# Second layer's feed-forward: the hidden levels of 15 of 16 tiles transposed by DMA instead of by TensorE

## The reference, cut to what matters

```python
def activation_quant(x, num_bits=8):
    s = qp / jnp.clip(jnp.max(jnp.abs(xf), axis=-1, keepdims=True), EPS, None)
    return (jnp.clip(jnp.round(xf * s), qn, qp) / s).astype(x.dtype)
def bit_linear(x, w):            # qx quantized by row, qw ternary
    return jnp.einsum('bsh,oh->bso', qx, qw)
h = jax.nn.silu(bit_linear(x, w_gate)) * bit_linear(x, w_up)     # 512 -> 2048
h = rms_norm(h, ln_weight)
return bit_linear(h, w_down)                                     # 2048 -> 512
x = x + ...
```

## Time and profile before

| what | us |
|---|---|
| median of three runs | 1560.83 |
| lowest, highest of them | 1557.06, 8537.07 |
| span of the profiled execution | 1560.6 |
| PE busy | 1503.3 (96%) |
| DVE busy | 1137.2 (73%) |
| ACT busy | 989.1 (63%) |
| POOL busy | 692.0 (44%) |

### The profile page before, as it was taken

One profiled execution on the slowest core, in us unless ns is written; L12 is line 12 of the kernel. 1 busy time (PEld: TensorE's weight loads), 2 busy tenths in 40 slices (PEclk: granted clock), 3 DMA queues, 4 the chain that ended last, 5 costly groups with the idle time before them and its releaser, 6 DMA issues. The chain is left out here.

```text
span 1560.6 us, 26693 instructions
## 1 busy us (share of the span) xinstructions
PE 1503.3 (96%) x8857; PEld 1178.0 (75%) x8899; DVE 1137.2 (73%) x2966; ACT 989.1 (63%) x2502; POOL 692.0 (44%) x832
## 2 busy tenths in 40 slices
PE   7899999999999999999999899999998799999988
PEld 6778888888888888888887666666666566666653
DVE  6787687777777777777788745555557888888774
ACT  5666666666666666666677755666666676666655
POOL 4565555555655555546476200000005355555544
PEclk9999999999999999999999999999999999999999
DMA  7011111111111111111336766666654301111000
GB/s 278 28 41 55 43 67 42 42 68 44 52 55 41 68 42 41 68 42 55 122 123 254 265 237 216 216 216 216 218 200 166 105 21 55 55 48 41 28 14 28
DMA packets 50538, 156.73 MB, mean 100 GB/s; under 512 B 5601, under 2 KB 5729, under 8 KB 48993
## 3 DMA queue, kind: packets, MB, share of 16 engines
q1 hardware_dynamic: 50400, 155.02, 28.1%
HBM read 113.05 MB, written 41.94 MB: 99 GB/s over the span
## 5 line engine op out<-in xcount | busy, mean ns | idle before, releaser
L617 ACT ACTIVATE Pt<-Pt,small 128x384 f32<-128x384 f32 (+1 forms) x256 | 172.8, 682 | 106.1 <-DVE small L877 106.0
L368 PE MATMUL bank<-wq,xT 128*128 128x512 f32 x768 | 206.7, 404 | 1.0 <-DVE wq L772 1.0
L421 PE MATMUL bank<-PT,vv 128*128 128x512 f32 x672 | 199.7, 406 | 5.3 <-DVE PT L862 4.5
L1135 POOL TENSOR_SCALAR Pt<-Pt,small 128x384 f32<-128x384 f32 (+1 forms) x256 | 164.2, 654 | 79.4 <-DVE small L885 79.4
L877 DVE CUSTOM_DVE_ANT_0 Pt<-quad,mask,small 128x384 f32<-128x384 f32 (+1 forms) x256 | 171.7, 680 | 30.7 <-PE quad L398 29.3
L1327 PE MATMUL bank<-wq,ot 128*128 128x512 f32 x768 | 189.9, 400 | 1.6 <-DVE xr L1514 1.4
L862 DVE TENSOR_TENSOR PT<-quad,PT 128x512 fp32r<-128x512 f32 x224 | 153.9, 687 | 37.9 <-ACT PT L609 37.5
L1327 PEld LDWEIGHTS bank<-wq,ot 128*128 128x128 f32 x768 | 143.3, 190 | 33.4 <-issue 1.9
L368 PEld LDWEIGHTS bank<-wq,xT 128*128 128x128 f32 x768 | 136.9, 189 | 26.2 <-DVE wq L772 2.3
L1123 POOL TENSOR_TENSOR t<-t 128x512 f32<-128x512 f32 x64 | 83.7, 1307 | 144.1 <-DVE t L843 144.0
L1629 POOL TENSOR_TENSOR cl<-cl,fixed 128x1 f32<-128x1 f32 x16 | 8.8, 550 | 296.7 <-DVE cl L1520 296.7
(11 more groups left out here) (289 smaller groups left out, 3553.3 us busy)
## 6 DMA issues: line engine op xcount, KB each, us to landing
ot_scratch<-OT SPq DMA_DIRECT2D x64, 512.0 KB, 2.8
ot<-ot_scratch SPq DMA_DIRECT2D x64, 512.0 KB, 3.4
wkv_f<-in_w SPq DMA_DIRECT2D x12, 512.0 KB, 6.4
wkc_f<-in_w SPq DMA_DIRECT2D x12, 512.0 KB, 6.5
wkv_f<-in_wg SPq DMA_DIRECT2D x11, 512.0 KB, 4.4
wkv_f<-in_wd SPq DMA_DIRECT2D x11, 512.0 KB, 4.8
wkv_f<-in_wu SPq DMA_DIRECT2D x10, 512.0 KB, 4.7
stg<-in_ctxT SPq DMA_DIRECT2D x16, 256.0 KB, 4.0
```

The source lines that it names most:

```text
L368: ins = pe.matmul(bQ[:], xT[p][:, k, qt * 128:qt * 128 + 128], wq[j][:, g, k, :], start=(part == 0 and k == 0), stop=(part == 2 and k == 3))
L421: ins = pe.matmul(bO[:], vv[x][:, bg % 2, kt, :], PT[y][:, k % 2, :], start=(kt == 0 and n == 0), stop=(kt == tiles_in(i) - 1 and n == 2))
L617: act.activation(p, p, ACT.Exp, bias=nm[:, i % 2, h:h + 1], scale=-1.0, accum_out=sm[:, i % 2, h:h + 1]).then_inc(f["s_exp"], 1)
L1135: pool.tensor_scalar(p, p, ri[:, i % 2, h:h + 1], 1.0, ALU.mult, ALU.mult).then_inc(f["p_n"], 1)
```

## The change

Each of the 15 tiles 0 to 14 is turned by two DMA transposes from the SP queue, one for each half of `bhh`, into a new SBUF buffer `bhL` (128 by 2048 float16). `act_hT` then reads `bhL` instead of a PSUM bank. Tile 15 keeps the turn on TensorE. The two transposes have semaphores of their own (two that the program's start had used and that stand at 32 and 16), the writers of `bhh` wait on them before they overwrite a half, and the transposes wait on h_tT before they overwrite a half of `bhL`. `pe_gate_up` has no turns inside any more. The waits on bank `bT` that stood for the turns are gone or name the earlier user; `pe_down` waits for x4 itself, since the turn that did so for it is gone. In SP's queue `sp_h_turn(n-1)` stands ahead of `sp_store(n-1)`, and `sp_h_turn(n)` behind the context loads and ahead of `sp_store(n)`.

```diff
+    hL = sb("bhL", [128, 2048], F16)
...
+    def sp_h_turn(n):
+        if n >= NT - 1:
+            return
+        for j in range(2):
+            sp.wait_ge(f[("hh_v", "hh_a")[j]], n + 1)
+            after(sp, f["h_tT"], 2 * n - 1 + j)
+            sp.dma_start_transpose(hL[:].rearrange("p (k n) -> p k n", k=16)[:, 8 * j:8 * j + 8, :],
+                                   hh[:, 1024 * j:1024 * j + 1024]).then_inc(f[f"b_ht{j}"], 16)
...
             if g_:
+                sp_h_turn(n - 1)
                 sp_store(n - 1)
...
             if f_:
+                sp_h_turn(n)
                 sp_store(n)
...
     def pe_xd(b):
         pe.wait_ge(f["pm"], 2 * b + 2)
-        if b >= 2:
-            pe.wait_ge(f["h_tT"], 2 * (2 * b - 3) + 1)
-        else:
-            pe.wait_ge(f["xat_lo"], min(2 * b + 4, NT))
-            after(pe, f["b_xq"], 1 if b == 1 else 0)
+        pe.wait_ge(f["xat_lo"], min(2 * b + 4, NT))
+        after(pe, f["b_xq"], 2 * b - 1)
...
-    def pe_gate_up(n, hook, q=None):
+    def pe_gate_up(n, q=None):
...
-            for m, part in hook:
-                if part[0] == j:
-                    pe_h_turn(m, part[1])
...
     def pe_down(n):
         pe.wait_ge(f["h_tT"], 2 * n + 2)
+        after(pe, f["x4"], n)
...
     def act_levels(n):
...
-        after(act, f["b_ht"], 2 * n)
+        after(act, f["b_ht1"], HT_BASE[1] + 16 * n if n else 0)
...
     def act_hT(n, j):
-        act.wait_ge(f["b_ht"], 2 * n + j + 1)
+        if n == NT - 1:
+            act.wait_ge(f["b_ht"], j + 1)
+            src = (bT, bM)[j][:].bitcast(F16)
+        else:
+            act.wait_ge(f[f"b_ht{j}"], HT_BASE[j] + 16 * (n + 1))
+            src = hL[:, j * 1024:j * 1024 + 1024]
```

More of the change, by code:

```diff
@@ L29 @@
 PRODUCTS = ((0, 0), (1, 0), (0, 1))
+HT_BASE = (32, 16)
 class Chain:
@@ L1895, in pe_x_turn @@
         else:
[L1896 to L1899, removed]
+            pe.wait_ge(f["xat_lo"], min(n + 6, NT))
+            pe.wait_ge(f["ap_lo"], n // 2 + 1)
             bank = bT[:].bitcast(F16)
@@ L1921, in pe_gate_up, with pe_h_turn @@
                 ins.then_inc(f["gu_mm"], 1)
-    def pe_h_turn(n, j):
-        pe.wait_ge(f["hh_a" if j else "hh_v"], n + 1)
-        b, odd = divmod(n, 2)
+    def pe_h_turn(j):
+        pe.wait_ge(f["hh_a" if j else "hh_v"], NT)
         if j == 0:
[L1927 to L1933, removed]
-        else:
-            pe.wait_ge(f["b_xq"], n + 1 + (1 - odd))
-            after(pe, f["x4"], n)
+            pe.wait_ge(f["b_xq"], NT)
+        else:
+            pe.wait_ge(f["x4"], NT - 1)
         bank = (bT, bM)[j][:].bitcast(F16)
@@ L1970, in pe_program @@
             if f_:
-                pe_gate_up(n, ((n - 1, (2, 0)), (n - 1, (3, 1))) if g_ else (), s if x_ else None)
+                pe_gate_up(n, s if x_ else None)
             elif g_:
@@ L1974, in pe_program @@
                 mem["pe_keep"](bA[0][:], 6)
-                pe_h_turn(n - 1, 0)
-                pe_h_turn(n - 1, 1)
+                pe_h_turn(0)
+                pe_h_turn(1)
                 mem["pe_keep"](bA[0][:], 5)
@@ L2003, in pe_program @@
             if f_:
-                pe_gate_up(n + 1, ((n, (1, 0)), (n, (2, 1))))
+                pe_gate_up(n + 1)
             if s == 1:
@@ L2107, in act_hT @@
     def act_hT(n, j):
-        act.wait_ge(f["b_ht"], 2 * n + j + 1)
+        if n == NT - 1:
[4 more added lines that the diff above has]
+            src = hL[:, j * 1024:j * 1024 + 1024]
         after(act, f["b_down"], n)
-        act.activation(hT[:, j * 1024:j * 1024 + 1024], (bT, bM)[j][:].bitcast(F16), ACT.Copy,
-                       bias=-MAGIC).then_inc(f["h_tT"], 1)
+        act.activation(hT[:, j * 1024:j * 1024 + 1024], src, ACT.Copy, bias=-MAGIC).then_inc(f["h_tT"], 1)
     def act_gate_up(n, hook, levels=None, q=None, m=None):
@@ L2499, in pool_levels @@
         pool.wait_ge(f["hw"], 4 * n + 4)
-        after(pool, f["b_ht"], 2 * n)
+        after(pool, f["b_ht0"], HT_BASE[0] + 16 * n if n else 0)
         pool.tensor_scalar(hh[:, 0:1024], hw[:, 0:1024], col(n)[:, 54:55], MAGIC,
@@ L2613, in block_kernel @@
         f = {n: top.enter_context(nc.semaphore(n)) for n in SEMAPHORES}
+        f["b_ht0"], f["b_ht1"] = f["x_first"], f["mask_in"]
         ot_dram = nc.dram_tensor("ot_scratch", (NT, 4, 128, 2, 512), F32, kind="Internal").ap()
```

## The result

The changed kernel takes 1573.62 us (median of four runs, 1572.98 to 1575.4), the kernel before 1559.17 us in the same comparison. The ratio is 1.0094 with an interval of 1.0080 to 1.0108: 14.5 us slower. The forecast was 1577 us, 16 us slower. The profiled execution has a span of 1571.6 us against 1560.6.

The account below looks back on a forecast made before the run. PE looked like the bound, but DVE set even tiles' group 3 and the landing would set odd down products. Terms 8.0, 2.1, 2.2, 2.9, 1.4, less 0.9 won, gave + 15.7 us on 1560.6: 1576, stated as 1577; range 1556 to 1607.

Parts of the forecast that it names:

- Turns leave PE: In gate/up, 30 turns, 13.2 us of PE time, go; even tiles' turns become waiting, except 0.88 us without DVE rounds.
- Turns go to DMA: Before odd down products: a steady odd tile costs max(a - 2.4, b - 4.6) us; five tiles, 5 x 1.6 = 8.0.
- a: Time from levels done to the first half landed as ACT sees it; taken as 4.0 us.
- b: Time from levels done to the second half landed as ACT sees it; taken as 6.0 us.
- ACT reads SBUF: ACT's two bhT instructions read SBUF in place of PSUM: 0.1 us each over seven odd tiles, 1.4 us.
- Tile 11: Before its down product: a - 1.1 and b - 3.3, less 0.8 us for PE's wait on DVE; 2.1 us.
- Tail: Tile 13's down product 2.2 us later; tile 14, where ACT's bhT blocks silu, a - 1.9 and b - 3.1, 2.9 us.
- The transposes are hidden: Rival: a near 2.0 and b near 2.5, every term at its floor, about - 3 us, 1557 us; chance 0.18.
- PE is the bound after all: Rival: the wait at group 3 is not the DVE's to keep, 13.2 us come back, 1547 us; chance 0.03.
- The queue takes them one by one: Rival: slow transposes one behind the other, a = 5.9, b = 11.8, 60 us slower, 1621 us; chance 0.26.
- The wait costs the clock too: Rival: PE's clock halves at seven waits before down products, 14 us on top, 1591 us; chance 0.06 alone.
- The two prices of the Trainium skill: For the landing: 256 KB under 1 us beside the fixed part, or 1309 ns a block, 10.5 us a half.

Follow-up runs that it names:

- the store behind: The changed kernel with the even tile's store issued behind the next odd tile's transposes and not ahead of them: 1574.72 us, ratio 1.0102.
- The last experiment: The changed kernel with tile 14, in the tail, turned on TensorE again: 1568.93 us, ratio 1.0074.
- the first experiment: The changed kernel with only even tiles 0 to 12 by DMA, all odd tiles and tile 14 turned on TensorE: 1556.62 us, ratio 0.9988.
- the third experiment: The changed kernel with one more transpose of half 0, into an unread buffer, ahead of the odd tiles' transposes; ACT waits for both: 1592.13 us, ratio 1.0209.
- ACT's other work first: The changed kernel with ACT's first bhT instruction of the odd tile moved behind silu and square of group 2: 1566.27 us, ratio 1.0051.

## Why the prediction was right, point by point

The sum was 15.7 us and the table gives 13.7. It was 2.4 us too high in the steady stages and 0.2 at each of the next two steps, and it had nothing for the last step, which gave 0.9. The path and its place were right; the sizes of several terms were not.

- *Turns leave PE.* Right. It said that the even tile's 0.88 us turn into waiting; the wait is 0.95 us, and fourteen transposes of even tiles changed a steady stage by nothing. The exception, the stage with no rounds on the DVE, was put at 0.9 us and gave 1.1.
- *Turns go to DMA.* Right in mechanism: the wait stands before the odd down product, ended by ACT's `bhT`, with ACT waiting for DMA at the first half. The stage was put at 44.2 us; two stages are 44.24, and the next three about 43.3.
- *What a and b are.* a was put at 4.0 us and measured 4.2, 4.2, 3.4, 3.3 and 3.3 us in the steady stages, so its mean, 3.7, was 0.3 below the forecast: over five stages this is 1.7 us of the 2.4 by which the sum of the steady stages came out below (6.6 for 9.0); the rest is the next point. b was put at 6.0 and is too large: SP issues the second transpose 1.3 us behind the first, and no second half cost a wait in the changed kernel. In the steady stages b did not set the forecast. At tile 14 it did (b - 3.1 = 2.9), and there a alone gives 1.4.
- *ACT reads SBUF.* Mis-sized: 0.1 us for each instruction was assumed, 1046 against 1023 ns was measured. The term of 1.4 us is worth 0.3.
- *Tile 11.* The prediction took off 0.8 us because PE waits for DVE work behind that down product. The step to tile 11 is 2.5 us longer, and the step from there to tile 12 is 1.3 shorter; the even tiles alone give 1.1 of that, so only 0.2 us came back. The sum still came out near (1.2 for 1.4) because a was 3.4 and not 4.0. That agreement is partly luck.
- *Tail.* The step from tile 12 to 14 was put at 5.3 us and is 5.07, but that the two are so near is luck. About 1.6 us of it is the clock, which the prediction had as a rival of its own and for which it thought a wait of some 2.5 us too short. After the wait of 2.58 us before tile 13's down product the windows show it:

```profile
1536.00:1538.00 2.00, 0.00 (x0) 0.00 (x0) 1.13 (x2) 2.00 (x5) 0.30 (x1) 1.00 0.00 0
1538.00:1540.00 2.00, 1.60 (x4) 0.59 (x5) 1.50 (x2) 1.74 (x5) 1.13 (x2) 0.56 0.00 0
1540.00:1542.00 2.00, 2.00 (x7) 0.76 (x6) 0.00 (x0) 0.52 (x2) 1.11 (x1) 0.58 0.00 0
```

  I take 1.6 us from the profile of the run with the store behind, where the step from tile 13 to 14 is 15.54 us in place of 17.13 and the clock fell behind the down product of tile 11 (and once more in the last step) instead:

```profile
1496.00:1498.00 2.00, 0.56 (x3) 0.31 (x4) 1.99 (x7) 2.00 (x5) 1.16 (x1) 0.99 0.00 0
1498.00:1500.00 2.00, 2.00 (x7) 0.69 (x5) 1.96 (x7) 0.72 (x3) 0.22 (x2) 0.50 0.00 0
```

  The split is an estimate from one pair of profiles. The last experiment bears it out: without a fall there and with tile 14 on TensorE the step is 14.15 us, which leaves 1.4 for tile 14's DMA, and the fall behind tile 11 costs 1.7 us in both runs that have it. So tile 13 was put at 2.4 us with its share of the point on SBUF and gave 2.1, while tile 14's 2.9 (from b) was 1.4, and the clock that the sum lacked made up for it.
- *The last step.* From tile 14 to 15 the prediction has no term, and 0.9 us are measured. The chain of waits there runs from the landing of tile 14's first half through ACT's silu and the DVE to the levels of tile 15. The same landing thus costs 1.4 us ahead of tile 14's down product and 0.9 behind it. With tile 14 back on TensorE both are gone.
- *Rivals.* "The transposes are hidden" came true for a copy, not for a transpose. "PE is the bound after all" fell with the first experiment. "The queue takes them one by one": the issues follow one another 1.3 us apart, not a landing apart, so it is out. "The wait costs the clock too" is true once in the changed kernel and at each of the seven odd tiles in the third experiment.
- *The two prices of the Trainium skill.* The 1309 ns for one block (the Trainium skill, VectorE: DVE Perf Modes, The three transpose paths) can't be multiplied by eight here: eight blocks land in 3.2 us together. The Trainium skill, Advanced Engine Details and Errata, DMA Advanced Topics, says that such a transpose is as fast as an ordinary transfer. For one transfer of 256 KB the runs don't agree: a plain copy lands in 2.4 us in the median, the transpose in 3.2, and in 4.2 at tiles 1 and 3. That difference decides the case.

## What to carry to other kernels

An engine can be busy for 98% of a stage, and a piece of work taken off it can still win nothing: look which wait ends at the next join, and whether the engine was waiting there already. A transfer in place of an instruction needs work ahead of it on every engine that waits in order, on the one that consumes it and on the one behind that; here moving one ScalarE instruction gave back 7 us of 14, and moving 12 matmuls 6. And choose it by place: the same DMA was free where its result was wanted 5 us later and cost 1 to 2 us where it was wanted in 2.4.

## What the runs showed of the hardware

- A DMA transpose of 128 by 1024 float16 from SBUF to SBUF keeps SP for 1.28 us in the median (a store 0.34, a plain copy of the same size 0.53). Over all profiles it lands in 3.0 to 5.1 us from its issue, a copy in 2.3 to 4.1. In the changed kernel the median is 3.2 us, but 4.2 at tiles 1 and 3; why is open.
- It is cut small: the page counts 82215 packets in place of 50538, 31677 more for 30 transposes, about 1056 for each, that is some 256 bytes a packet. The HBM traffic is unchanged.
- The clock fell to half (1.2 of 2.4 GHz) at each of the seven odd tiles of the third experiment, behind PE waits of 3.0 to 4.0 us. With shorter waits their length does not tell: it fell behind 2.58 us (tile 13, changed kernel), 2.18 and 2.24 us (tile 11, the store behind and the tail's tile back), and 2.47 us (tile 14, ACT's other work first), and stayed at 1.00 behind 2.50 us (tile 3) and 2.38 us (tile 11) in the changed kernel and behind 2.71 us (tile 13, the tail's tile back). What else decides is not shown.
